# Selective-scan block: the projections beside the scan in products of 512 columns, spread over more steps

## What is computed

```python
xs, z = jnp.split(h @ in_w, 2, axis=-1);  xs = silu(xs)
proj = xs @ xproj_w
dt = softplus(proj[..., :D_INNER] + dt_bias)
Bm, Cm = proj[..., D_INNER:D_INNER + D_STATE], proj[..., D_INNER + D_STATE:]
def step(hst, ins):
    dA = exp(dt_t[:, :, None] * A)
    hst = hst * dA + (dt_t * x_t)[:, :, None] * B_t[:, None, :]
    return hst, einsum('bds,bs->bd', hst, C_t)
out = (ys + xs * Dskip) * silu(z) @ out_w
```

## Time and profile before

| | us |
|---|---|
| median of 3 runs | 5379.84 (5379.78 to 5382.82) |
| the profiled execution | 5380.16 |
| its span, first to last instruction | 5378.4 |
| PE busy | 4902.5 (91%) |
| DVE busy | 4725.0 (88%) |
| ACT busy | 3391.5 (63%) |
| POOL busy | 3758.3 (70%) |
| mean granted TensorE clock | 0.981 of 2.4 GHz |

### The profile page before, as it was taken

One profiled execution on the slowest core, in us unless ns is written; L12 is line 12 of the kernel. 1 busy time (PEld: TensorE's weight loads), 2 busy tenths in 40 slices (PEclk: granted clock), 3 DMA queues, 4 the chain that ended last, 5 costly groups with the idle time before them and its releaser, 6 DMA issues. The chain is left out here.

```text
span 5378.4 us, 130410 instructions
## 1 busy us (share of the span) xinstructions
PE 4902.5 (91%) x44784; PEld 2509.1 (47%) x44784; DVE 4725.0 (88%) x2419; ACT 3391.5 (63%) x11482; POOL 3758.3 (70%) x6613
## 2 busy tenths in 40 slices
PE   6999999898989999898999999898999999886898
PEld 4544444454544444454544444454544444443444
DVE  2989899999999998999989899999999999997443
ACT  4767667676767666676767667676767667563111
POOL 4777777777787877787777777777777877775211
PEclk8999999999999999999999999999999999998999
DMA  3111111111111111111111112111111111112452
GB/s 105 51 49 51 59 37 61 41 51 52 52 51 49 59 37 60 41 51 49 53 50 50 54 39 64 41 51 49 53 50 46 59 37 43 35 27 93 153 158 66
DMA packets 433144, 306.74 MB, mean 57 GB/s; under 512 B 215921, under 2 KB 336241, under 8 KB 432497
## 3 DMA queue, kind: packets, MB, share of 16 engines
q1 hardware_dynamic: 428272, 294.39, 18.1%
q10 hardware_dynamic: 4224, 4.19, 0.2%
HBM read 187.27 MB, written 111.15 MB: 55 GB/s over the span
## 5 line engine op out<-in xcount | busy, mean ns | idle before, releaser
L866 DVE TENSOR_TENSOR_SCAN b_hs<-b_dA,b_u 128x1024 f32<-128x1024 f32 x2048 | 4538.7, 2271 | 291.5 <-ACT b_u L793 207.4
L1021 PE MATMUL b_ex<-b_dd,b_aw 32*128 32x512 f32 x8192 | 2688.8, 648 | 50.2 <-ACT b_dA L775 21.8
L1008 PE MATMUL b_u<-b_ud,b_bw 32*128 32x256 f32 x16384 | 2354.9, 403 | 318.0 <-DVE b_hs L866 300.8
L775 ACT ACTIVATE b_dA<-b_ex 128x496 f32<-128x496 f32 x4096 | 2294.8, 590 | 156.6 <-PE b_ex L1021 152.4
L1008 PEld LDWEIGHTS b_u<-b_ud,b_bw 32*128 32x128 f32 x16384 | 1448.9, 186 | 1197.2 <-issue 689.8
L1040 PE MATMUL b_y<-b_hs,b_cw 128*32 128x256 f32 x16384 | 1320.9, 393 | 2.3 <-DVE b_hs L866 2.3
L525 POOL TENSOR_TENSOR b_dd<-b_dr,b_mask 128x512 f32<-128x512 f32 x1024 | 1074.9, 1050 | 224.5 <-DVE b_hs L866 209.6
L793 ACT ACTIVATE b_u<-b_hin 128x32 f32<-128x32 f32 x1792 | 365.7, 204 | 1300.4 <-PE b_u L1008 1056.7
L534 POOL TENSOR_TENSOR b_ud<-b_ur,b_mask 128x512 f32<-128x512 f32 x1024 | 1085.4, 1060 | 0.1
L561 POOL TENSOR_TENSOR b_hm<-b_first,b_hs 128x32 f32<-128x32 f32 x1792 | 483.6, 270 | 573.7 <-ACT b_first L774 550.7
L1021 PEld LDWEIGHTS b_ex<-b_dd,b_aw 32*128 32x128 f32 x8192 | 834.9, 185 | 90.5 <-ACT b_dA L775 52.9
(11 more groups left out here) (106 smaller groups left out, 2217.9 us busy)
## 6 DMA issues: line engine op xcount, KB each, us to landing
b_u<-scratch_ut SPq DMA_DIRECT2D x256, 128.0 KB, 2.9
scratch_y<-b_ysb SPq DMA_DIRECT2D x128, 256.0 KB, 2.3
scratch_xs<-b_xs SPq DMA_DIRECT2D x64, 256.0 KB, 2.1
scratch_sz<-b_sd SPq DMA_DIRECT2D x64, 256.0 KB, 2.2
scratch_dt<-b_sd SPq DMA_DIRECT2D x64, 256.0 KB, 2.0
scratch_ut<-b_uT SPq DMA_DIRECT2D x64, 256.0 KB, 2.3
b_ur<-scratch_ut SPq DMA_DIRECT2D x1024, 16.0 KB
b_dr<-scratch_dt SPq DMA_DIRECT2D x1024, 16.0 KB, 1.7
```

The lines of the kernel that those rows point to most:

```text
L775: nc.scalar.activation(dA[:, j % NDA, h, :, 1:TC], src[:, :, 1:TC], ACT.Exp).then_inc(exp_done, 1)
L866: nc.vector.tensor_tensor_scan(hs[:, v, :, :, kp].rearrange("p d t -> p (d t)"), dA[:, j % NDA, :, :, :].rearrange("p h d t -> p (h d t)") ...
L1008: ins = nc.tensor.matmul(dst[:, :, tb, :], bw[row(r), c % 2, tb, :], ud[row(r), j // 2 % NPR, tb, :, :], start=(tb == 0), stop=(tb == NTB ...
L1021: nc.tensor.matmul(e[bank_of[what]][:, :], aw[row(r), p % DIRS, v, :, :].rearrange("p b s -> p (b s)"), dd[row(r), (p * PAIRS + j // 2) % ...
```

## The change

Each xz and dt product now takes both batches at once (512 columns, a whole bank) and is issued one instruction at a time. The pieces of one xz product are two steps apart and the next product follows three steps on. The four pieces of a dt product come at 0, 2, 5 and 7 of 16 steps. B and C keep 256 columns, in two steps three apart. Only five xz products come ahead of dt; the last three (z of channels 128 to 511) come after it, and so do their stores and the load of the next `win` on SP. A job's bank is held for 4 steps (xz), 9 (dt) or 5 (B and C), by the spans given to `job_slots`. ACT takes 512 columns at a time, one instruction a step, and loads an activation table three times a unit, not twice. `pre` has two buffers, `nd` is gone, and `normalise` stands between the softplus parts. Statistics move from step 64 to 32.

```diff
-        DT_JOB = (16, 20, 24, 27)
-        UT_JOB = (22, 26, 29, 30)
-        BC_JOB, BT_JOB, UNIT_JOBS = 18, 23, 31
-        DT_SLOT = (48, 60, 72, 84)
-        BC_SLOT, BT_SLOT = 54, 69
+        XZ_JOB = (0, 1, 2, 3, 4, 15, 17, 18)
+        DT_JOB = (5, 7, 9, 12)
+        XZ_SLOT, XZ_SPAN = (0, 5, 10, 15, 20, 89, 100, 105), 4
+        DT_SLOT, DT_SPAN = (25, 41, 57, 73), 9
+        BC_SLOT, BC_SPAN = (35, 51), 5
+        UT_SLOT, UT_SPAN = (67, 83, 86, 97), (4, 4, 2, 1)
+        TURN_SLOT, TURN_SPAN = (112, 116), 2
...
-                def project_xz(q, i, b):
+                def project_xz(q, i):
                     bank_free(n)
                     for k in range(MB):
-                        last = nc.tensor.matmul(job_bank(n)[:, 0:SEQ], win[:, k, i * P:(i + 1) * P],
-                                                hT[:, q % DIRS, k, b * SEQ:(b + 1) * SEQ], start=(k == 0), stop=(k == MB - 1))
+                        ins = nc.tensor.matmul(job_bank(n)[:, :], win[:, k, i * P:(i + 1) * P], hT[:, q % DIRS, k, :],
+                                               start=(k == 0), stop=(k == MB - 1))
+                        if k == 0:
+                            yield from wait_steps(2)
...
+                def project_dt(q, j):
                     bank_free(n)
                     for k in range(JB):
+                        ins = nc.tensor.matmul(job_bank(n)[:, :], wxp[:, k, j * P:(j + 1) * P], xs[:, k, :],
+                                               start=(k == 0), stop=(k == JB - 1))
+                        if k + 1 < JB:
+                            yield from wait_steps(3 if k == 1 else 2)
...
-                    for i in range(SILUS):
-                        for b in range(CB):
-                            project_xz(q, i, b)
-                            yield from wait_steps(3)
+                    for i in range(JB + 1):
+                        yield from project_xz(q, i)
+                        yield from wait_steps(3)
```

More of the change, by code:

```diff
@@ L113, in main_phase @@
         sd = sb("b_sd", [P, JB, T])
-        pre = sb("b_pre", [P, T])
+        pre = sb("b_pre", [P, 2, T])
         ey = sb("b_ey", [P, T])
@@ L352, in unit @@
                     put_ut(3)
+                    put_sz(1)
+                    put_sz(2)
+                    if q + 1 < PASSES:
+                        hold(sp, sp_passed, full, base + UNIT_JOBS)
+                        load_win(q + 1)
+                    put_sz(3)
                     yield
@@ L680, in take_bc @@
                 def take_bc(q, b):
[L681 removed]
+                    n = first_job(q) + BC_JOB[b]
                     act.wait_ge(full, n + 1)
@@ L698, in unit @@
                 def unit(q):
+                    c = q // DIRS + 1
+                    norm_next = q % DIRS == 1 and q + 1 < PASSES
                     nc.scalar.preload_act_table_set("exp_and_others")
-                    for i in range(SILUS):
-                        take_xz(q, i, 0)
-                        yield from wait_steps(3)
-                        take_xz(q, i, 1)
+                    for i in range(JB + 1):
+                        yield from wait_steps(2)
+                        yield from take_xz(q, i)
@@ L727, in unit @@
+                        yield from take_dt(q, j)
+                        if j == 0:
+                            nc.scalar.preload_act_table_set("natural_log_exp_and_others")
+                        logs = log_part(q, j)
+                        for _ in range(4):
                             yield
                             next(logs, None)
-                            yield from wait_steps(2)
-                            take_bt(q)
-                            yield from wait_steps(3)
-                        elif j == 2:
-                            take_ut(q, 1)
-                            yield
-                            next(logs, None)
-                            yield from wait_steps(5)
+                        yield
@@ L743, in unit @@
-                    if q % DIRS and q + 1 < PASSES:
-                        c = q // DIRS + 1
-                        yield from wait_steps(2)
-                        root(c)
-                        yield from wait_steps(7)
+                        yield
+                        if norm_next and j == 1:
+                            root(c)
+                        yield
+                    nc.scalar.preload_act_table_set("exp_and_others")
+                    yield from wait_steps(2)
+                    yield from take_xz(q, JB + 1)
@@ L928, in project, with project_bc @@
+                    ins.then_inc(full, 1)
+                def project_bc(q, b):
+                    n = first_job(q) + BC_JOB[b]
+                    bank_free(n)
+                    for k in range(JB):
+                        ins = nc.tensor.matmul(job_bank(n)[:, 0:SEQ], wxp[:, k, DI:PW], xs[:, k, b * SEQ:(b + 1) * SEQ],
                                                start=(k == 0), stop=(k == JB - 1))
                         if k == 1:
-                            yield
+                            yield from wait_steps(3)
```

223 lines of the change are left out of this document (109 added, 114 removed).

## The result

| kernel | time, us | ratio to the kernel before |
|---|---|---|
| before | 5381.33, median of 4 runs (5379.78 to 5386.94) | 1 |
| changed | 5551.16, median of 4 runs (5548.54 to 5555.48) | 1.0315, 95% interval 1.0302 to 1.0328 |

The change costs 170 us. The forecast was 103 more, 5483, with 5440 to 5515 as its most likely stretch and 5555 as its outer bound: the direction and, for most of it, the place were right, the size was not. The measured time is 4 us inside that outer bound. The profiled execution of the changed kernel has a span of 5546.8 us, against 5378.4.

The account below looks back on a forecast made before the run. Scans set the floor (2.18 us each); side work uses PE's reserve, which held exponents remove. Eight passes at 309.2 and seven at 311.2 make 4652 against 4541.3, +111, less 8 ahead of the scans: 5483 us; likely 5440 to 5515, range 5390 to 5555.

Parts of the forecast that it names:

- 41 to 88 hardly changed: Sign in pass 3: steps 41 to 56 at 39.6 us against 39.35, steps 57 to 88 at 78.0 against 79.5.
- stays, once a dt product: POOL's standstill at `softplus` (248.8 us, 64 times), making ACT wait 242.1 us for the carry, was to remain.
- POOL, costed at 0: `times_sigmoid` one step behind `plus_one`: 2.8 us of lead hides it; 0, at most 0.5 us a product.
- The rival that had POOL at 3 us a pass: `times_sigmoid` and late SP stores add 3 us to each pass: 5530 us; chance 0.18.
- The hold: Exponents held by two alternating banks, plus pieces: pass 3 sums to 307.7 us against 298.0, with 1.5 added: 309.2.
- The rule: With two banks, PE's gap to the next step is max(1.65, 4.34 - previous gap), plus 1.06 us for a piece.
- I add 0.3 for each of two such places: dt cycle of 16 steps: exponents held 1 us reach ACT late, raising 39.0 us to 39.6.
- The normalising passes: Seven passes: the exponent's wait for `modulate` goes, DVE statistics stay; 2 us above the others, 311.2 us each.
- Ahead of the first scan: Unit 0, from two `pre` buffers and fewer xz products before dt: 8 us saved, bounds 0 and 15.
- spreading works: Rival: exponents do not wait for banks, spread pieces vanish, a pass takes 281 us: 5050 in all; chance 0.09.
- the long piece is cheap: Rival: a 512-column piece costs 0.86 us, about 5.7 us less a pass: 5398; chance 0.08.
- waits overlap: Rival: side costs fall into one another and worse spacing only cancels the gains: 5360 to 5391 us; chance 0.05.

## Why the forecast was right, and where its size was off

*Direction.* Right, and by the cause named. PE saves nothing by longer products (1.06 us a piece, measured twice), and exponents held by their banks take PE's reserve away. That the hold costs much is shown: one number of bank reservation costs the kernel before 162 us. Shorter holds, with closer pieces, give the changed kernel 91 back. With POOL's work late in both kernels the change costs 5472.79 - 5284.03 = 189 us, more than the 170 of the two as they stand. For the kernel before had a stall of its own, at `softplus`, which the changed kernel no longer has. Steps 41 to 88 of pass 3, for the changed kernel and then for the kernel before, both with late POOL:

```profile
1131.93:1250.49 118.56, 106.75 (x49) 1.00 0.18 51
1093.19:1208.49 115.30, 107.17 (x49) 1.00 0.20 57
```

Without the late POOL work they take 118.6 and 118.9. So the forecast's "41 to 88 hardly changed" came true by two things that cancel: the stall of `softplus` went, 3.5 us a pass, and the holds and places cost 3.3. The forecast had it that this stall "stays, once a dt product"; POOL does still wait there (167.9 us), but the scans lose nothing by it in these steps. That part of the agreement is luck.

*The sum.* The forecast had 4652 us for the 15 passes, and they took 4712. Term by term:

- **POOL, costed at 0.** This is the step that failed: "POOL's order gives 2.8 us of lead, which hides it while steps take 2.4 us". The lead was read off the order, but POOL itself runs ahead of ACT until it meets its own wait, and then the diagonals and carries behind it are as late as ACT. Moved two steps on, it gives 78 us back. The rival that had POOL at 3 us a pass (5530) was the right addition and still too small: 5.2. Without this term the 15 passes take 4632 us, 20 below the forecast.
- **The hold.** With POOL out of the way pass 3 takes 309.0 us, against a sum of 307.7 and an added 1.5. Its sections: 38.06 for 37.6, 63.66 for 62.8, 51.62 for 52.6. The agreement is partly luck. The rule's "I add 0.3 for each of two such places" was about 0.5 in each (steps 41 to 56 took 40.14 where the cycles alone give 39.0), and where the case comes in every cycle, as in the kernel before with long holds, the rule foretold 70 us of 162. It falls short where a held step follows a held one, and it leaves out the `add_up` of every eighth step.
- **The normalising passes.** Forecast 2 us above the others; measured none (312.5 for pass 4, 314.2 for pass 3). Seven of them: 14 us too many in the forecast.
- **Ahead of the first scan.** 5.8 us saved, for 8.
- **Behind the last scan.** 3.3 us more, not forecast and not followed up.

*The rivals.* That spreading works fell: two plain held steps do fit into 4.36 us, but only as long as no piece comes. That the long piece is cheap fell with the 1.06. (The forecast's 0.215 us for 256 columns was half of rows 6, not read from rows 5, which have 1.06 for four products together.) On this the Trainium skill, "TensorE: Matmul & The Clock Gate", section "Back-to-back issue gap", has lower cost per column for long products in a stream; the trace doesn't bear it out for these fp32 products, and the measurement decides. That waits overlap was half true without changing the side: the 105 us in front of every eighth scan were worth 15.

*What was to be seen.* Step starts 1.06 us behind a piece, steps 0 to 15 and 16 to 40 longer, 41 to 88 hardly changed (by the luck told above) and pass 15 at 276.7 all came. The wait for ACT's `decay` was 201 us rather than several hundred, and the first scan at 103.1 rather than 101. Steps 89 to 110, where the forecast expected 52.6, are where a reader of the new profile should have stopped first.

*Left open.* The places and the hold overlap, and their split in the whole kernel isn't known beyond steps 0 to 15; the close pieces were not run with the long hold. How much of POOL's cost is the fallen clock and how much the wait itself is only estimated.

## What to carry to other kernels

A wait that stands one step behind its producer in an in-order queue can delay everything queued behind it, even on an engine that is idle a third of the time; see first whether moving it back gives time, and compare two versions only with such stalls out of both. Where operations share a few PSUM banks, count the steps for which each bank is taken, from the first write to the last read: longer products that save no time per column can cost more in banks than they give. Hold and extra work must be priced together: in steps 0 to 15 here a held step was free until a piece stood in it.

## What the runs showed of the hardware

The granted clock fell at very short stops. PE had idled no longer than 1.02 us at a time, with 0.98 of 2 us and then 1.39 of 2 us busy, and the next 4 us had a mean of 0.58 of full speed; `add_up` took 1.06 us instead of 0.64. The Trainium skill, "TensorE: Matmul & The Clock Gate", section "HAM oscillation — how this bites in real kernels", describes such falls behind waits for DMA that are longer than these. Here shorter stops were enough, in a kernel whose PE is busy 94% of its span.

In the scans of the kernel before, the stretches at the lower level add up to 101 us, and `softplus` two steps later on another engine took them to 12.

An fp32 product cost the same per column at 256 and at 512 columns (1.06 us a piece in both forms), entering and leaving included.
